# DLRM tower with a three-layer CIN: cur0's sums as six fp32 products and one fp32r product, and the next x transposed at other slots

## Chip, cores and metric

One core of one Trainium2 chip. The metric is the device time of one execution in microseconds (us). Engines: PE (TensorE), DVE (VectorE), ACT (ScalarE), POOL (GpSimd), and SP, which issues DMAs only. The page of the profile and the rows below come from one profiled execution.

## The reference, cut to what matters

```python
# B=1024 rows, 39 fields of D=16; e: (1024, 39, 16), gathered from 39 tables
x0 = e; xk = e; outs = []
for W in (f0, f1, f2):                       # (39*39,128), (128*39,128), (128*39,128)
    z = einsum('bfd,bgd->bfgd', x0, xk).reshape(b, f*g, d)
    cur = einsum('bpd,pm->bmd', z, W)        # cur0, cur1, cur2: (b, 128, 16)
    outs.append(cur); xk = cur
z = sum(concatenate(outs, axis=1), axis=-1)  # (b, 384)
h = concatenate([z, dense_ctx], axis=1)      # (b, 400)
h = relu(h @ W_top1 + b_top1)                # 512
h = relu(h @ W_top2 + b_top2)                # 256
y = h @ W_top3                               # (b, 1)
```

All of it is float32. The change concerns cur0 = the sum over pairs (f, g) of x_f x_g f0[f, g]. As x_f x_g = x_g x_f, the kernel adds f0[f, g] and f0[g, f] once and has 39 x 20 pairs in place of 39 x 39: field f with field f + s (mod 39), for the shifts s = 0 to 19.

## The kernel before, in words

**Tiling.** The 1024 rows are 8 batch tiles (bt) of 128 rows. Each has four groups (q = 0 to 3) of 32 rows, so there are 32 groups g (NG), each with 32 x 16 = 512 columns (row, dimension). A group has four tiles j of 128 columns, and a tile ten chunks c, of four fields each (the tenth has three). TensorE goes through the 40 slots s of a group (s = 10 j + c). In each slot it does one chunk of layer 1: `cur0` of the tile against four fields of f1, 512 columns, as three products of high and low fp32r parts (lines 842 to 844). Six PSUM banks go round: ACT scales the chunks c = 0, 2, 4, 5, 7, 8 by x (line 538), and DVE fuses scaling and sum for c = 1, 3, 6, 9 (lines 681 and 688). DVE adds up the tile (lines 700 and 707) into a ring `cur1` of eight tiles.

**What is laid between the chunks**, at slots written out by hand: the G products of the group before (slot 12, line 799), the seven sums of cur0 for the group after (slots 13, 16, 19, 22, 25, 28, 31, `AT_SUM`, line 770), layer 2 (line 806), the MLP, and in groups with q = 2 the transposes of the next batch tile's x (c = 5 of each tile, so slots 5, 15, 25 and 35, line 744) which ACT reads (line 504). At slot 39 stand the transposes that make x a scale per partition (line 757, ACT line 509).

**cur0.** The partitions hold three blocks of 39 fields (117 rows). Block j of `base` is x moved by -7 j. Copy k (k = 0 to 6) is x moved by k. Their product holds the shifts k, k + 7 and k + 14, so that seven K-tiles cover the 20 shifts (the seventh has two blocks, 78 rows). To make x movable, `x_seq` has 123 rows: the 39 fields three times and six of them once more. SP issues for each group three copies to `base` and six to `shifted` (lines 315 and 324), all from SBUF to SBUF. GpSimd multiplies `shifted` by `base` (line 427) into a ring of three `pairs`, seven times per group, laid between its gathers of the rows of the next batch tile (line 391): three in tile 0, two in tile 1, two in tile 2. TensorE multiplies them by `f0_sum` in fp32 (line 770) into the bank C. In the fourth tile ACT rounds C to the high part of cur0 (line 515), and DVE takes the low part and the sum over the dimension (lines 656 and 658). For group 0 DVE makes the pairs (line 652).

**Queues around it.** GpSimd also copies the gathered rows in field order (line 405), in groups with q = 1: two parts ahead of its pairs in the third tile and two in the fourth. `pair` waits for the sum that frees its place in the ring. SP waits with a copy until the pairs that read the old one are made, and at q = 0 until ACT has read all four transposes of the new x (`x_read`).

## Time and profile before

| | us |
|---|---|
| median of 3 runs | 1350.27 (1345.81 to 1350.93) |
| the profiled execution | 1340.59 |
| its span, first to last instruction | 1338.9 |

| engine | busy us of the span |
|---|---|
| PE | 1274.2 |
| PE weight loads | 979.7 |
| DVE | 1079.9 |
| ACT | 1050.2 |
| POOL | 662.8 |

The granted TensorE clock has a mean of 0.983 of full speed and is below 0.95 only in the first tenth of the span. How to read it: the rows until about 83 us are start (gathers, weights, cur0 of group 0), then come the 32 groups, and the last 20 us are the tail of layer 2 and the MLP. In a timeline, matmuls are pipelined and their ends are modelled, so only the distance from start to start is a price. Idle time of an engine stands in brackets with what ended it.

### The profile page before, as it was taken

To read this page: it belongs to the slowest core of one execution; us is meant where nothing else is said; L and a number is where in the kernel's file an instruction comes from. 1 tells how busy PE (TensorE), PEld (TensorE's weight loads), DVE (VectorE), ACT (ScalarE), POOL (GpSimd) and SP (SyncE) were. 2 spreads that over 40 slices of the span, in tenths; PEclk is the share of its full clock that TensorE was granted. 3 is DMA by queue.
4 is the path that set the end of the run, shared out by engine and by line. 5 is a ranking of instruction groups with operands and counts; after the bars stand their busy time and mean duration, and the time that the engine had idled before them with its cause. 6 is when DMAs were issued, how large, how long until landed. Compare 5 with 4: busy or idle time off the path is not lost. (4 is left out here: it accounts for less than half of the span.)

```text
span 1338.9 us, 21410 instructions
## 1 busy us (share of the span) xinstructions
PE 1274.2 (95%) x6680; PEld 979.7 (73%) x6680; DVE 1079.9 (81%) x2285; ACT 1050.2 (78%) x3363; POOL 662.8 (50%) x634
## 2 busy tenths in 40 slices
PE   1389999999999999999999999999999999999998
PEld 0357777777787777777777777777777777777787
DVE  2059989988889888788878888898887888788884
ACT  2058888888888888788878888888887888788884
POOL 7787556654545557454466545455474532233100
PEclk8689999999999999999999999999999999999999
DMA  5073022100311013110211103111031102110000
GB/s 142 11 196 98 21 58 67 52 28 3 104 33 38 28 29 88 44 32 14 73 51 51 29 3 98 32 44 29 20 90 50 31 13 70 49 49 27 1 1 1
DMA packets 51177, 63.60 MB, mean 48 GB/s; under 512 B 13067, under 2 KB 24344, under 8 KB 51019
## 3 DMA queue, kind: packets, MB, share of 16 engines
q1 hardware_dynamic: 34544, 56.08, 13.7%
q0 software_dynamic: 10128, 2.98, 2.1%
q10 hardware_dynamic: 6392, 3.18, 0.9%
q8 instruction: 53, 0.87, 0.3%
q14 instruction: 60, 0.49, 0.1%
HBM read 11.08 MB, written 1.02 MB: 9 GB/s over the span
## 5 line engine op out<-in xcount | busy, mean ns | idle before, releaser
L538 ACT ACTIVATE scaled_x<-Y,x_col 128x128 f32<-128x128 f32 x3072 | 929.8, 506 | 190.4 <-PE Y L844 178.8
L842 PE MATMUL Y<-f_high,cur_high 128*128 128x512 f32 (+1 forms) x1280 | 603.9, 472 | 3.7 <-DVE sum_b L688 2.0
L844 PE MATMUL Y<-f_high,cur_low 128*128 128x512 f32 (+1 forms) x1280 | 499.1, 390 | 0.0
L843 PE MATMUL Y<-f_low,cur_high 128*128 128x512 f32 (+1 forms) x1280 | 499.0, 390 | 0.0
L427 POOL TENSOR_TENSOR pairs<-shifted,base 117x512 f32<-117x512 f32 x186 | 241.8, 1302 | 435.9 <-PE C L770 434.0
L688 DVE SCALAR_TENSOR_TENSOR sum_a<-Y,x_col,sum_a 128x128 f32<-128x128 f32 x768 | 264.8, 345 | 155.6 <-PE Y L844 153.4
L391 POOL DMA_INDIRECT rows<-in_tbl_dram,ids_sb x312 | 306.6, 983 | 77.5 <-issue 65.9
L842 PEld LDWEIGHTS Y<-f_high,cur_high 128*128 128x128 f32 x1280 | 241.3, 189 | 95.8 <-issue 37.2
L843 PEld LDWEIGHTS Y<-f_low,cur_high 128*128 128x128 f32 x1280 | 242.2, 189 | 86.2 <-issue 52.1
L707 DVE TENSOR_REDUCE cur<-scaled_x 128x128 f32<-128x1920 f32 x128 | 275.6, 2153 | 15.0 <-ACT scaled_x L538 1.6
L844 PEld LDWEIGHTS Y<-f_high,cur_low 128*128 128x128 f32 x1280 | 240.7, 188 | 51.1
L770 PE MATMUL C<-pairs,f_sum 117*128 117x512 f32 (+1 forms) x448 | 236.1, 610 | 5.5 <-DVE pairs L652 5.0
L700 DVE TENSOR_REDUCE scaled_x<-scaled_x 128x128 f32<-128x1536 f32 x128 | 223.4, 1745 | 0.0
L688 DVE SCALAR_TENSOR_TENSOR sum_b<-Y,x_col,sum_b 128x128 f32<-128x128 f32 x640 | 219.2, 342 | 0.0
L770 PEld LDWEIGHTS C<-pairs,f_sum 117*128 117x128 f32 (+1 forms) x448 | 83.0, 193 | 40.6 <-ACT G L521 13.0
L806 PEld LDWEIGHTS C<-G,f_sb 128*128 128x128 f32 x624 | 82.6, 191 | 6.4 <-DVE G L718 0.8
L806 PE MATMUL C<-G,f_sb 128*128 128x128 f32 x624 | 83.3, 275 | 0.7 <-ACT G L521 0.7
L427 POOL TENSOR_TENSOR pairs<-x_seq,base 117x512 f32<-117x512 f32 x31 | 40.0, 1289 | 76.3 <-DMA base<-x_seq 75.2
L688 DVE SCALAR_TENSOR_TENSOR scaled_x<-Y,x_col,sum_b 128x128 f32<-128x128 f32 x128 | 59.8, 467 | 0.0
L688 DVE SCALAR_TENSOR_TENSOR scaled_x<-Y,x_col,sum_a 128x128 f32<-128x128 f32 x128 | 57.7, 451 | 0.0
L681 DVE TENSOR_SCALAR sum_a<-Y,x_col 128x128 f32<-128x128 f32 x128 | 43.9, 343 | 5.7 <-PE Y L844 5.7
L681 DVE TENSOR_SCALAR sum_b<-Y,x_col 128x128 f32<-128x128 f32 x128 | 43.8, 342 | 0.0
(90 smaller groups left out, 730.6 us busy)
## 6 DMA issues: line engine op xcount, KB each, us to landing
shifted<-x_seq SPq DMA_DIRECT2D x157, 234.0 KB
base<-x_seq SPq DMA_DIRECT2D x95, 78.0 KB
rows<-in_tbl_dram,ids_sb POOLq DMA_INDIRECT x312
shifted<-x_seq SPq DMA_DIRECT2D x31, 156.0 KB
G<-in_L_rec_f_dram ACTq DMA_DIRECT2D x3, 832.0 KB, 8.6
w_sb<-in_W_top_dram SPq DMA_DIRECT2D x1, 768.0 KB
f_ext<-in_L_rec_f_dram SPq DMA_DIRECT2D x1, 760.5 KB
w_sb<-in_W_top_dram SPq DMA_DIRECT2D x1, 512.0 KB
```

Source lines behind the costliest of these rows:

```text
L391: pool.indirect_dma_start(out=rows[:, f * D:(f + 1) * D], out_offset=None, in_=tables[f], in_offset=bass.IndirectOffsetOnAxis(ap=ids_sb[:, ...
L427: pool.tensor_tensor(pairs[0:r, z % RING, :], shift, base[0:r, g % 2, :], ALU.mult)\
L538: ins = act.activation(scaled_x[:, :, PLACE[c] + i], where[:, i * M:(i + 1) * M], ACT.Copy, scale=x_col[:, t // JT % QG, t % JT, f:f + 1])
L681: dve.tensor_scalar(acc, src, x, None, ALU.mult).then_inc(acc_steps, 1)
L688: dve.scalar_tensor_tensor(to, src, x, acc, ALU.mult, ALU.add).then_inc(acc_steps, 1)
L700: dve.tensor_reduce(scaled_x[:, :, FIRST_SUM], scaled_x[:, :, 0:HALF], AX.X, ALU.add).then_inc(acc_steps, 1)
L707: dve.tensor_reduce(cur1[:, t % CUR1_RING, :], scaled_x[:, :, FIRST_SUM:PLACES], AX.X, ALU.add).then_inc(acc_steps, 1)
L770: pe.matmul(C[:], f0_sum[0:r, k, :], pairs[0:r, z % RING, :], start=k == 0, stop=k == K0 - 1).then_inc(cur0_summed, 1)
L806: ins = pe.matmul(C[:, 0:P], f2_sb[:, f, :], half[:, f, :], start=f == first, stop=f == end - 1)
L842: pe.matmul(where, ch, wh, start=True, stop=False)
L843: pe.matmul(where, ch, wl, start=False, stop=False)
L844: pe.matmul(where, cl, wh, start=False, stop=True).then_inc(y_filled, 1)
```

## The change

cur0 of group g (from 1 on) is made from six K-tiles and one further product:

- Block j of `base` is now moved by -6 j, and copies k = 0 to 5 give the shifts 0 to 17 with 117 rows. The shifts 18 and 19 are left.
- Rows 117 to 127, 11 rows which were free, hold a part of them: in the copies k = 0 to 3 they carry the pairs of fields 21 to 31 with fields k to k + 10, which are 18 or 19 apart. `x_seq` and `rows_seq` grow to 128 rows, `base` gets a fourth copy (11 rows).
- The last 40 pairs (four runs of ten) are gathered in `base_left` and `left_pairs` by eight copies of ten rows; once these have landed, four copies of 40 rows repeat them twice: 120 rows. GpSimd multiplies them ("left"), ACT rounds them to fp32r (`left_high`, slot 24), GpSimd puts the low part in rows 0 to 39 ("low"). Against them stand f0 as high, high, low. So one fp32r product gives low x high + high x high + high x low. It takes the place of the seventh sum (slot 31).
- GpSimd's order is now three pairs in tile 0, three in tile 1, "left" and "low" in tile 2. The ring of pairs goes on through groups with six uses (`ring_uses`).
- In group 0 the shifts 18 and 19 are a seventh fp32 product with 78 rows, from two copies that GpSimd issues.
- At the start SP loads f0 in 22 DMAs in place of 10, ACT loads 24 pieces for the last product, and DVE makes its high and low parts in four operations.
- The transposes of the next x go from slots 5, 15, 25, 35 to 5, 15, 19, 23 (`AT_X`), and ACT's reads with them.
- For room in SBUF, the ring of `cur1` has 6 tiles and not 8, and DVE waits at each of its tiles for the G product that read the old one; `y`, `z2` and `y_col` lie in `h1`, `h2` and `block`.

```diff
-K0 = -(-SHIFTS // BLK)
+KT = SHIFTS // BLK
+FAR = BLK * KT
+K0 = KT + 1
+EXTRA = P - SEL
+FAR_TILES, FAR_FIELD = 4, NF - FAR
+ROWS = [P - k if k < FAR_TILES else SEL for k in range(KT)]
+FIRST_ROWS = [SEL] * KT + [2 * NF]
+LEFT_FIELD, LEFT_PARTNER, LEFT_RUNS = EXTRA, EXTRA + FAR, 4
+LEFT_N = FAR_FIELD - LEFT_FIELD
...
-AT_X = 5
+AT_MLP2 = 5
+AT_X = (5, 15, 19, 23)
+AT_LEFT_HIGH = 24
-CUR1_RING = 2 * JT
+CUR1_RING = JT + 2
...
                 if g >= 3:
-                    sp.wait_ge(pairs_ready, K0 * (g - 2))
+                    sp.wait_ge(pairs_ready, KT * (g - 2))
...
                 for j in range(BLK):
                     base_copy(sp, g, j)
-                for k in range(1, K0):
+                sp.dma_start(base[SEL:P, g % 2, :], cols[FAR_FIELD:FAR_FIELD + EXTRA, :]).then_inc(based[g % 2], 16)
+                for k in range(1, KT):
                     if g >= 2:
-                        sp.wait_ge(pairs_ready, K0 * (g - 2) + k + 1)
+                        sp.wait_ge(pairs_ready, KT * (g - 2) + k + 1)
                     shift_copy(sp, g, k)
+                if g >= 2:
+                    sp.wait_ge(left_low_ready, g - 1)
+                for r in range(LEFT_RUNS):
+                    rows_r = slice(LEFT_N * r, LEFT_N * (r + 1))
+                    f, v = LEFT_FIELD, LEFT_PARTNER + r
+                    sp.dma_start(base_left[rows_r, :], cols[f:f + LEFT_N, :]).then_inc(left_copied, 16)
+                    sp.dma_start(left_pairs[rows_r, :], cols[v:v + LEFT_N, :]).then_inc(left_copied, 16)
+                sp.wait_ge(left_copied, 16 * (LEFT_COPIES * (g - 1) + 2 * LEFT_RUNS))
+                for j in (1, 2):
+                    rows_j = slice(j * LEFT_PAIRS, (j + 1) * LEFT_PAIRS)
+                    sp.dma_start(base_left[rows_j, :], base_left[0:LEFT_PAIRS, :]).then_inc(left_copied, 16)
+                    sp.dma_start(left_pairs[rows_j, :], left_pairs[0:LEFT_PAIRS, :]).then_inc(left_copied, 16)
...
+            def left_products(g):
+                pool.wait_ge(left_copied, 16 * LEFT_COPIES * g)
+                pool.tensor_tensor(left_pairs[:], left_pairs[:], base_left[:], ALU.mult).then_inc(left_made, 1)
+
+            def left_low(g):
+                n = LEFT_PAIRS
+                pool.wait_ge(left_high_ready, g)
+                pool.tensor_tensor(left_x[0:n, :], left_pairs[0:n, :], left_x[0:n, :].bitcast(F32), ALU.subtract)\
+                    .then_inc(left_low_ready, 1)
...
-                    ks = ((0, 1, 2), (3, 4), (5, 6), ())[j] if g + 1 < NG else ()
+                    ks = ((0, 1, 2), (3, 4, 5), ("left", "low"), ())[j] if g + 1 < NG else ()
...
+            def left_high(g):
+                act.wait_ge(left_made, g)
+                if g >= 2:
+                    act.wait_ge(cur0_summed, K0 * g)
+                act.activation(left_x[:], left_pairs[:], ACT.Copy).then_inc(left_high_ready, 1)
...
-                        if c == AT_X:
-                            if q == 2 and bt + 1 < BT:
-                                read_transposes(bt + 1, j)
-                            if with_mlp:
-                                relu2(mlp, mlp + 1)
+                        if CH * j + c in AT_X and q == 2 and bt + 1 < BT:
+                            read_transposes(bt + 1, AT_X.index(CH * j + c))
+                        if CH * j + c == AT_LEFT_HIGH and g + 1 < NG:
+                            left_high(g + 1)
+                        if c == AT_MLP2 and with_mlp:
+                            relu2(mlp, mlp + 1)
...
-                if j == 0 and g >= 2:
-                    dve.wait_ge(s_filled, S_USE["G", g - 2] + 1)
+                if t >= CUR1_RING:
+                    dve.wait_ge(s_filled, S_USE["G", (t - CUR1_RING) // JT] + 1)
...
+            dve.wait_ge(left_f0_in, 16 * 6 * LEFT_RUNS)
+            dve.tensor_tensor(left_f0[:, 0, :], left_f0[:, 0, :], left_f0[:, 1, :], ALU.add).then_inc(left_f0_ready, 1)
+            dve.wait_ge(left_f0_ready, 1)
+            dve.tensor_copy(f0_left[:], left_f0[:, 0, :]).then_inc(left_f0_ready, 1)
+            dve.wait_ge(left_f0_ready, 2)
+            dve.tensor_tensor(f0_left[64:LEFT, :], left_f0[64:LEFT, 0, :], f0_left[64:LEFT, :].bitcast(F32),
+                              ALU.subtract).then_inc(left_f0_ready, 1)
+            dve.wait_ge(left_f0_ready, 3)
+            dve.tensor_copy(f0_left[64:2 * LEFT_PAIRS, :], left_f0[64:2 * LEFT_PAIRS, 0, :]).then_inc(left_f0_ready, 1)
...
                 if k == 0 and g:
                     pe.wait_ge(c_read, C_USE["sum", g])
-                if g:
-                    pe.wait_ge(pairs_ready, z - K0 + 1)
+                if g and k == KT:
+                    pe.wait_ge(left_low_ready, g)
+                    if g == 1:
+                        pe.wait_ge(left_f0_ready, 4)
+                    w, x = f0_left[:], left_x[:]
                 else:
-                    pe.wait_ge(first_pairs, k + 1)
-                r = K0_ROWS[k]
-                pe.matmul(C[:], f0_sum[0:r, k, :], pairs[0:r, z % RING, :],
-                          start=k == 0, stop=k == K0 - 1).then_inc(cur0_summed, 1)
+                    if g:
+                        pe.wait_ge(pairs_ready, KT * (g - 1) + k + 1)
+                        r = ROWS[k]
+                    else:
+                        pe.wait_ge(first_pairs, k + 1)
+                        r = FIRST_ROWS[k]
+                    w, x = f0_sum[0:r, k, :], pairs[0:r, RING_USE[g, k] % RING, :]
+                pe.matmul(C[:], w, x, start=k == 0, stop=k == K0 - 1).then_inc(cur0_summed, 1)
...
-                    if c == AT_X and q == 2 and bt + 1 < BT:
-                        transposes(bt + 1, j)
+                    if s in AT_X and q == 2 and bt + 1 < BT:
+                        transposes(bt + 1, AT_X.index(s))
```

## Rows read from the trace of the kernel before

**Rows 1.** The page's first part: busy us (share of the span), instructions.
```profile
PE 1274.2 (95%) x6680; PEld 979.7 (73%) x6680; DVE 1079.9 (81%) x2285; ACT 1050.2 (78%) x3363; POOL 662.8 (50%) x634
```
**Rows 2.** Windows: stretch, length, busy of PE, PEld, DVE, ACT, POOL; PEclk, DMA, GB/s.
```profile
680.00:720.00 40.00, 40.00 (x220) 31.27 (x219) 33.07 (x70) 32.84 (x109) 20.66 (x21) 1.00 0.15 41
```
**Rows 3.** Waits, weight loads in 130 to 1285, GpSimd in all: total, times, longest.
```profile
PEld Y L842 <- DVE sum_b L688: 4.1, 11, 1.1
...
POOL pairs L427 <- DMA base<-x_seq: 75.2, 7, 17.0
```
**Rows 4.** Timeline of TensorE, a group with q = 1: start, us, operation.
```profile
603.28 1.02 PE L770 MATMUL C<-pairs,f_sum 117*128 117x512 f32 x2
603.74 0.80 PE L842 MATMUL Y<-f_high,cur_high 128*128 128x512 f32 x1
604.38 0.40 PE L843 MATMUL Y<-f_low,cur_high 128*128 128x512 f32 x1
604.61 0.40 PE L844 MATMUL Y<-f_high,cur_low 128*128 128x512 f32 x1
...
606.06 1.02 PE L770 MATMUL C<-pairs,f_sum 78*128 78x512 f32 x2
606.52 0.79 PE L842 MATMUL Y<-f_high,cur_high 128*128 128x512 f32 x1
607.15 0.40 PE L843 MATMUL Y<-f_low,cur_high 128*128 128x512 f32 x1
```
**Rows 5.** Timeline of GpSimd, the same group.
```profile
592.73 1.30 POOL L427 TENSOR_TENSOR pairs<-shifted,base 117x512 f32<-117x512 f32 x1 [0.53 <-PE C L770]
...
595.46 0.95 POOL L391 DMA_INDIRECT rows<-in_tbl_dram,ids_sb  x1 [0.31 <-issue]
597.73 2.52 POOL L405 COPY rows_seq<-rows 128x624 f32<-128x624 f32 x2 [1.33 <-DMA rows<-in_tbl_dram,ids_sb]
```
**Rows 6.** Timeline of ACT, the same group, tiles 2 and 3.
```profile
599.12 2.71 ACT L538 ACTIVATE scaled_x<-Y,x_col 128x128 f32<-128x128 f32 x8 [0.97 <-PE Y L844]
602.09 2.70 ACT L538 ACTIVATE scaled_x<-Y,x_col 128x128 f32<-128x128 f32 x8 [0.25 <-PE Y L844]
605.04 2.53 ACT L538 ACTIVATE scaled_x<-Y,x_col 128x128 f32<-128x128 f32 x8 [0.26 <-PE Y L844]
607.34 0.67 ACT L515 ACTIVATE cur_high<-C 128x512 fp32r<-128x512 f32 x1
```
**Rows 7.** Timeline of TensorE: sums 1 and 2, and the next group's first product.
```profile
591.63 1.02 PE L770 MATMUL C<-pairs,f_sum 117*128 117x512 f32 x2
...
594.59 1.02 PE L770 MATMUL C<-pairs,f_sum 117*128 117x512 f32 x2
...
613.36 1.05 PE L806 MATMUL C<-G,f_sb 128*128 128x128 f32 x8
```
**Rows 8.** Timeline of DVE: tile 2's sum, and its read of C in tile 3.
```profile
606.68 2.15 DVE L707 TENSOR_REDUCE cur<-scaled_x 128x128 f32<-128x1920 f32 x1
...
611.41 0.69 DVE L658 TENSOR_REDUCE z<-C 128x32 f32<-128x512 f32 x1
```
**Rows 9.** Timeline of TensorE, the group with q = 3: the sum at slot 31.
```profile
683.82 1.02 PE L770 MATMUL C<-pairs,f_sum 78*128 78x512 f32 x2
```
**Rows 10.** Timeline of ACT, the same group: slots 22 and 24.
```profile
676.88 2.71 ACT L538 ACTIVATE scaled_x<-Y,x_col 128x128 f32<-128x128 f32 x8 [0.97 <-PE Y L844]
```
**Rows 11.** Timeline of SP's queue, the copies for the next batch tile's first group.
```profile
652.12 2.35 SPq L315 DMA_DIRECT2D base<-x_seq  x3
```
**Rows 12.** Timeline of GpSimd: the pair that waited for these copies.
```profile
656.23 1.29 POOL L427 TENSOR_TENSOR pairs<-x_seq,base 117x512 f32<-117x512 f32 x1 [9.61 <-DMA base<-x_seq]
```
**Rows 13.** Timeline of DVE at the start.
```profile
60.00 0.72 DVE L631 COPY rows_seq<-rows 128x624 f32<-128x624 f32 x1 [30.88 <-DMA rows<-in_tbl_dram,ids_sb]
...
82.11 0.69 DVE L656 TENSOR_TENSOR cur_low<-C,cur_high 128x512 fp32r<-128x512 f32 x1 [3.66 <-ACT cur_high L515]
```
**Rows 14.** Timeline of ACT at the start.
```profile
60.00 1.31 ACT L487 ACTIVATE rows_seq<-rows 128x624 f32<-128x624 f32 x1 [38.21 <-DMA rows<-in_tbl_dram,ids_sb]
```

More of the change, by code:

```diff
@@ L29, with ring_uses @@
 BLK = P // NF
-K0 = -(-SHIFTS // BLK)
-K0_ROWS = [NF * sum(k + K0 * j < SHIFTS for j in range(BLK)) for k in range(K0)]
+KT = SHIFTS // BLK
+FAR = BLK * KT
+K0 = KT + 1
 SEL = BLK * NF
-SEQ = SEL + K0 - 1
-ROW_PARTS = [(0, NF), (NF, NF), (2 * NF, NF), (SEL, SEQ - SEL)]
+ROW_PARTS = [(0, NF), (NF, NF), (2 * NF, NF), (SEL, P - SEL)]
+EXTRA = P - SEL
[4 more added lines that the diff above has]
+LEFT_N = FAR_FIELD - LEFT_FIELD
+LEFT_PAIRS = LEFT_RUNS * LEFT_N
+LEFT = 3 * LEFT_PAIRS
+LEFT_COPIES = 2 * LEFT_RUNS + 4
 RING = 3
+def ring_uses():
+    uses = [(0, k) for k in range(K0)] + [(g, k) for g in range(1, NG) for k in range(KT)]
+    return {u: n for n, u in enumerate(uses)}, [K0 * g + k for g, k in uses]
 CH = 10
@@ L256, in build @@
         f1_cuts = [13, 26, 39]
-        EXT = NF + K0 - 1
+        EXT = NF + KT - 1
         f0_ext = nc.dram_tensor("f0_ext", (EXT, EXT, M), F32).ap()
-        F0_EXT, F0_LOADS = 3, 2 * (2 * BLK - 1)
+        FAR_RUNS = []
+        for j, (u, v) in enumerate(((0, FAR), (NF - KT, FAR + 1 - KT))):
+            row = 0
+            while row < NF:
+                n = min(NF - row, NF - u, EXT - v)
+                FAR_RUNS.append((NF * j + row, n, u, v))
+                row, u, v = row + n, (u + n) % NF, (v + n) % NF
+        F0_EXT, F0_LOADS = 3, 2 * (2 * BLK - 1) + 2 + 2 * len(FAR_RUNS)
         def extend_f0(eng):
@@ new lines, in load_f0, with load_left_f0 @@
+            for row, n, u, v in FAR_RUNS:
+                eng.dma_start(f0_sum[row:row + n, KT, :], f0_rows(u, v, n)).then_inc(f0_in, 16)
+                eng.dma_start(f0_mirror[row:row + n, KT, :], f0_rows(v, u, n)).then_inc(f0_in, 16)
+        def load_left_f0(eng):
+            for j in range(3):
+                for r in range(LEFT_RUNS):
+                    row = j * LEFT_PAIRS + r * LEFT_N
+                    u, v = LEFT_FIELD, LEFT_PARTNER + r
+                    eng.dma_start(left_f0[row:row + LEFT_N, 0, :], f0_rows(u, v, LEFT_N)).then_inc(left_f0_in, 16)
+                    eng.dma_start(left_f0[row:row + LEFT_N, 1, :], f0_rows(v, u, LEFT_N)).then_inc(left_f0_in, 16)
@@ L455, in _ @@
                             take_rows(bt + 1, part)
[L456 removed]
+                    ks = ((0, 1, 2), (3, 4, 5), ("left", "low"), ())[j] if g + 1 < NG else ()
                     for i in range(max(len(ks), len(fs))):
                         if i < len(ks):
[L459 removed]
+                            if ks[i] == "left":
+                                left_products(g + 1)
+                            elif ks[i] == "low":
+                                left_low(g + 1)
+                            else:
+                                pair(g + 1, ks[i])
                         if i < len(fs):
```

130 lines of the change are left out of this document (74 added, 56 removed).

## The prediction

> **What bounds the kernel now.** First the page's busy shares: TensorE is busy for 1274.2 of 1338.9 us, DVE 1079.9, ACT 1050.2, GpSimd 662.8 [rows 1]. A share is an average, so the second view is a stretch in the middle: from 680 to 720 us TensorE is busy for all 40 us at a granted clock of 1.00, while DVE has 7 us, ACT 7 us and GpSimd 19 us free [rows 2]. Third, the waits: between 130 and 1285 us the weight loads waited for DVE at most 1.1 us in one place and 4.1 us in 11 [rows 3]. So from about 83 us on the row of products on TensorE is the time, and what leaves that row shortens the run as long as the others keep up. They have room on average, but not at every moment, and the change spends that room.
>
> **The product that is replaced.** Starts in TensorE's timeline are pitches. Within a chunk an fp32r product of 512 columns and 128 rows follows the last after 604.61 - 604.38 = 0.23 us. From the start of a cur0 sum (603.28) to the second product of the next chunk (604.38) there are 1.10 us, which hold the fp32 sum and one fp32r product: the sum costs 0.87 us. The seventh sum, with 78 rows, costs 607.15 - 606.06 - 0.23 = 0.86 us: rows don't matter, only columns and type [rows 4]. The durations printed (1.02 for two records) overlap their neighbours and aren't used.
> After the change, groups 1 to 31 have six fp32 sums (128 or 117 rows, same price) and one fp32r product of 120 rows and 512 columns. I price it at 0.23, from its nearest row, the fp32r product of 128x512. Bounds: 0.23 below (it can't stream fewer columns) and 0.86 above (no gain, if the switch of type cost all that was saved). I take the lower end, since chunks follow sums in the same manner already and the switch is inside the 0.86. Saved: 31 x (0.86 - 0.23) = 19.5 us. Group 0 keeps seven fp32 products, the seventh with 78 rows as before: 0.
>
> **The new chain beside it.** The fp32r product needs its pairs as high and low parts: GpSimd multiplies (left), ACT rounds at slot 24, GpSimd subtracts (low), TensorE reads at slot 31. On GpSimd two operations replace one of 1.30 us [rows 5], +1.3 us in a group with 19 us free: nothing. On ACT there is one more pass over 512 columns, about 0.67 us like the split of cur0 at 607.34 [rows 6], in a group with 7 us free. But both are waits in queues. Behind ACT's wait stand the scalings of slots 25, 27 and on, which free TensorE's banks and feed DVE; behind GpSimd's wait for ACT stand gathers, copies of rows and the next group's pairs.
> The tightest place is a group with q=1, where GpSimd copies two parts of the next rows before it comes to left. Before: a pair starts 1.10 us after the sum that frees its place (592.73 [rows 5] against 591.63); sum 2 starts at 594.59 [rows 7]; the last gather is issued at 595.46 and the copies begin at 597.73, when it has landed, 1.3 us after its end [rows 5]. After: pair 5 comes ahead of that gather, 595.7 to 597.0; gather 597.1 to 598.1; landed 599.4; two copies, 602.0; left, 603.25. ACT is done with slot 24 at 599.12 + 2.71 = 601.8 [rows 6], waits 1.5 us and rounds until 603.9; low is ready at 605.2. TensorE asks for it at slot 31, at 606.06 [rows 4]: 0.8 us to spare, no direct wait. Indirectly: ACT's slot 28, which ended at 606.2 (half of the eight from 605.04 [rows 6]), ends at about 607.3, so DVE's sum over the tile starts at 607.4 instead of 606.68, and all behind it moves by 0.7 us. DVE's read of C ends at 612.8 instead of 612.1 [rows 8], while TensorE, 0.63 us sooner, wants to begin the next group at 613.36 - 0.63 = 612.7 [rows 7]: 0.1 us of waiting, bounds 0 and 1.5 (ACT's whole wait passed on). For 8 groups 0.8 us, bounds 0 and 12. Group 1 has one gather more in that tile (1.25 us), which uses up the 0.8: 0.4 us more.
> In the other groups no copy stands there. In the one with q=3, slot 31 is at 683.82 and so sum 2 at 672.35; pair 5 until 674.8, one gather, left 675.9 to 677.2; ACT is done with slot 24 at 679.6 [rows 9, 10] and rounds until 680.3, low 681.6. That is 2.4 us to spare for ACT and 2.2 for TensorE, and ACT's gaps of 0.25 us at slots 25 and 28 take up most of the rounding: 0.
>
> **SP's queue.** Per group it issued 9 copies and will issue 21, at 0.78 us each (2.35 for three [rows 11]). The new 12 come in two steps: 8 small copies (10 rows each), a wait for their landing, 4 of 40 rows. From the issue of a copy to GpSimd's release there are 2.5 us (third base copy at 653.7, GpSimd at 656.23 [rows 12]), so the chain takes 8 x 0.78 + 2.5 + 4 x 0.78 + 2.5 = 14.4 us. It starts when low of the group before is done (605) and is wanted one group later at 637 (675.9 less a pitch of 38.9, half of 683.82 - 606.06): 17 us to spare, 0. Behind it in the queue are the base copies of the group after, wanted later still.
> The Trainium skill (DMA: Bandwidth & Descriptors, the sections Rules for kernel authors and Anatomy of one DMA) speaks against this part: transfers under 64 KB are mostly overhead, with about 2.0 us fixed for each, and should be joined. If the twelve came one after another at that price they would take 24 us, an estimate by that page. The 0.78 us between issues in this trace shows that copies overlap.
> Here the moved transposes matter. Their cost on TensorE is the same wherever they stand. With the fourth at slot 35, SP began the next x's copies at 652.12; slot 23 is 12 chunks (0.70 us), three sums and a transposition sooner, 11.4 us, so 640.7. Nine copies, 7 us, and the small ones, 14.4 us, are done at 662, wanted at 675.9. Unmoved it would be 673.5. So the move gives no time itself, it keeps the chain covered. GpSimd's waits for base copies (75.2 us in 7 places [rows 3]) should go; nobody on the path waited for them. The transposes of slot 19 need ACT's read of those of slot 15: bound one pass, 0.67 us x 7, taken as 0. The shorter ring of cur1 (6) makes DVE wait for the products of group g-1 only at the end of the third tile, some 10 us after they were made: 0.
>
> **Start and end.** SP has 12 more loads of f0 (at 0.78 us 9 us) and ACT 24 small ones (19 us); DVE and ACT sat idle until the rows came at 60.00, for 30.9 and 38.2 us [rows 13, 14]: nothing. DVE makes the high and low weights in four small operations where it sat idle for 3.66 us before its split of cur0 [rows 13]: nothing. GpSimd issues three copies for group 0 instead of two: bounds 0 and 0.78, I take 0.3. For group 1, SP begins after the last pair of group 0, at 78.5, and has the small copies in at 99.9; left comes 7.9 us before slot 31, which is near 109, so at 101: 0, though with little to spare. The tail is the same.
>
> **Sum.** 19.5 - 0.8 - 0.4 - 0.3 = 18.0 us. The profiled execution took 1340.59 us (span 1338.9), so it would take 1322.6. The median of the three runs is 1350.27, 9.7 us above it with the same program, which the trace doesn't explain. I forecast against the median: **1332 us**.
>
> **Rivals.** (1) The hand-over GpSimd, ACT, GpSimd is late in the q=1 groups by 1 to 2 us beyond the margin of 0.8: TensorE stands at slot 31 in 8 groups, 8 to 16 us: 1340 to 1348. For it: the copies of rows stand ahead; against: the pieces are measured. (2) The fp32r product is dearer, in itself or by the switch of type inside one accumulation, which no row shows: halfway, at 0.55 us, 10 us are lost, 1342; at 0.86, 1351. (3) Slower: the hand-over is late in every group. The margin at slot 31 is 2.2 us, and once TensorE waits over 0.63 us in each group the kernel is slower than before, so from 2.9 us late on; at 4 us late 31 x 1.8 - 19.5 = +36 us, 1386. It takes a chain of small copies of 34 us and not 14. Against it: 17 us to spare there and 19 us of GpSimd's time free [rows 2].
>
> **How the numbers follow.** Forecast 0.76 (1321 to 1338: the sum against the profiled execution and against the median, with stalls of 0 to 6 us), rival 1 0.11, rival 2 0.08, rival 3 0.05. The range of 1321 to 1343 takes in half of rivals 1 and 2. A measurement of this kernel tells about 0.5% (6.8 us) from no change: under 1343.5 lie the forecast, over half of 1 and half of 2, 0.87; same 0.08; slower 0.05.
>
> **What would show it.** In the changed profile: starts around the seventh product 0.23 us apart; slot 31 to slot 31 over two groups 76.5 us (77.76 before); no wait of TensorE for GpSimd at slot 31; a wait of ACT of 1 to 2 us before the rounding in q=1 groups alone; none of GpSimd for base copies; chunks starting at 83 us still. Wrong it is if TensorE waits at slot 31, if ACT's wait shows in all groups, or if the seventh product is well over 0.23.

## The result, and the profile after

The changed kernel takes **1360.27 us** (median of 7 runs, 1355.68 to 1364.74); the kernel before, on the same chip, 1346.62 us (7 runs, 1344.99 to 1353.85). The ratio is **1.0092 [1.0071, 1.0113]**: slower, by about 12 to 14 us, where 18 us of gain were forecast. The profiled execution of the changed kernel took 1355.68 us, with a span of 1354.0 us (1340.59 and 1338.9 before).

The page's first part of the changed kernel (busy us, share of the span, instructions), to be read beside [rows 1]:

```profile
PE 1268.2 (94%) x6649; PEld 975.1 (72%) x6649; DVE 1080.0 (80%) x2290; ACT 1053.5 (78%) x3394; POOL 706.4 (52%) x666
```

TensorE has less work and the span is 15.1 us longer, so TensorE must have stood still. Its timeline around slot 31 of a group shows first that the product is not at fault (start, us, operation; starts are pitches):

```profile
663.50 0.39 PE L958 MATMUL Y<-f_high,cur_low 128*128 128x512 f32 x1
663.73 0.40 PE L885 MATMUL C<-left_x,f_left 120*128 120x512 f32 x1
663.97 0.40 PE L956 MATMUL Y<-f_high,cur_high 128*128 128x512 f32 x1
```

The next product starts 663.97 - 663.73 = 0.24 us after it, against 0.86 for the sum it replaces [rows 4]. The waits between 130 and 1285 us (total, times, longest) say where TensorE stands:

```profile
POOL pairs L501 <- DMA shifted<-x_seq: 51.6, 9, 12.2
...
ACT left_x L612 <- POOL left_pairs L506: 25.3, 7, 11.4
...
POOL rows_seq L479 <- DMA rows<-in_tbl_dram,ids_sb: 18.8, 7, 5.1
...
PE C L885 <- POOL left_x L511: 9.0, 1, 9.0
```

One stop of 9.0 us at slot 31, ACT late seven times, and a line that the forecast had not thought of: GpSimd waits 51.6 us in nine places for a copy to `shifted`. (The waits of its pairs for copies to `base` [rows 3] are gone but for one of 1.7 us, as forecast.) To place the loss I took the starts of the transposes of slot 39 (the chunks' groups end there) in both timelines and subtracted the distances:

| stretch, after minus before, us | profiled run | same kernel, later set |
|---|---|---|
| up to the first chunks (81 us) | +2.2 | -1.0 |
| group 0 | +3.0 | +3.7 |
| group 1 | +13.4 | +13.1 |
| the seven later groups with q = 1 | +2.0 | +2.2 |
| the other 21 groups from group 2 to 29 | -6.6 | -9.5 |

So the change works in most groups (about 0.5 to 0.6 us each), loses in the groups with q = 1, and loses most in two groups at the start. (Of the seven later groups with q = 1 six lose 0.4 to 0.5 us each; the seventh belongs to the last batch tile, has no next rows to copy, and gains 0.55.) The stretch before the chunks differs by some us between executions of kernels with the same code in it (-3.2 to +5.5 in the runs below), and I explain nothing by it.

**Group 1.** SP's queue in the changed kernel, the copies for group 1's pairs (start, us in the queue):

```profile
82.61 0.74 SPq L414 DMA_DIRECT2D base<-x_seq  x1
83.39 8.80 SPq L379 DMA_DIRECT2D shifted<-x_seq  x5
92.23 0.73 SPq L424 DMA_DIRECT2D base_left<-x_seq  x1
```

Five copies take 8.80 us to issue. Half of that is the second one, of 126 rows, which stands behind the one of 127 rows:

```profile
84.09 4.27 SPq L379 DMA_DIRECT2D shifted<-x_seq  x1
```

In the kernel before six of them at the same place take 4.79, that is 0.80 each:

```profile
80.93 4.79 SPq L324 DMA_DIRECT2D shifted<-x_seq  x6
```

What moved in the meantime stands in the DMA view, in 40 equal parts of the stretch 84 to 90 us (digits: busy tenths of the 16 DMA engines), first the changed kernel, then the kernel before in 84 to 97 us:

```profile
DMA  3120100001000200001013313010000005686885
GB/s 68 41 24 4 41 14 14 14 27 14 0 0 27 27 0 0 0 27 27 0 27 44 41 31 34 27 34 27 27 27 27 27 14 164 191 246 218 287 273 123
```
```profile
DMA  4587787788979837999999999999999999999999
GB/s 140 126 251 252 246 284 284 233 265 277 265 240 103 76 107 230 290 323 347 334 290 302 296 284 302 284 309 290 290 290 301 295 254 284 291 296 290 265 287 259
```

After the first slice, for almost 5 us, the 16 engines move 0 to 44 GB/s between them, though a copy of 254 KB is under way and four more wait to be issued; before, 230 to 347 GB/s are usual (weights among them). In the stretch 84.7 to 89.0 us the same view gives for SP's queue (packets, MB, share of the 16 engines):

```profile
q1 hardware_dynamic: 36, 0.07, 6.4%
```

6.4% of 16 engines is one engine. The copy of 127 rows was issued at 83.39, and GpSimd, which waits for nothing else, can use it 14 us later (timeline of GpSimd, groups 0 and 1; in brackets the idle time and what ended it):

```profile
97.38 1.29 POOL L501 TENSOR_TENSOR pairs<-shifted,base 127x512 f32<-127x512 f32 x1 [7.39 <-DMA shifted<-x_seq]
...
136.92 1.30 POOL L501 TENSOR_TENSOR pairs<-shifted,base 127x512 f32<-127x512 f32 x1 [8.04 <-DMA shifted<-x_seq]
...
156.80 2.40 POOL L479 COPY rows_seq<-rows 128x624 f32<-128x624 f32 x2 [5.08 <-DMA rows<-in_tbl_dram,ids_sb]
159.17 1.25 POOL L506 TENSOR_TENSOR left_pairs<-left_pairs,base_left 120x512 f32<-120x512 f32 x1
161.16 1.26 POOL L511 TENSOR_TENSOR left_x<-left_pairs,left_x 40x512 fp32r<-40x512 f32 x1 [0.74 <-ACT left_x L612]
```

254 KB in 14 us are 19 GB/s. The pairs that GpSimd makes in group 1 come late too. Its copies for them stand in SP's queue behind the loads of the weights of layer 2 and the MLP; they go out at 119.53 us, and in a kernel that loads these weights two groups later (weights_later, below) at 102.59:

```profile
119.53 2.47 SPq L370 DMA_DIRECT2D base<-x_seq  x3
```
```profile
102.59 2.35 SPq L370 DMA_DIRECT2D base<-x_seq  x3
```

Then the copy of 127 rows takes its 14 us again, and GpSimd idles 8.04 us for it. So the last gather is issued late and lands late, and behind it stand the two copied parts of the next rows, then left, ACT's rounding and low. ACT waits 11.4 us with the banks of Y full, and TensorE stands:

```profile
160.45 0.63 ACT L612 ACTIVATE left_x<-left_pairs 120x512 fp32r<-120x512 f32 x1 [11.39 <-POOL left_pairs L506]
```
```profile
162.48 0.80 PE L885 MATMUL C<-left_x,f_left 120*128 120x512 f32 x1 [9.04 <-POOL left_x L511]
163.07 0.63 PE L956 MATMUL Y<-f_high,cur_high 128*128 128x512 f32 x1
163.50 0.63 PE L957 MATMUL Y<-f_low,cur_high 128*128 128x512 f32 x1
```

The stop has a second price. After it products follow each other by 163.50 - 163.07 = 0.43 us instead of 0.23: TensorE's clock had fallen to its lower level (1.2 GHz) while it stood; from 163 to 167 us the granted clock is 0.50. The windows (stretch; length, busy of PE, PEld, DVE, ACT, POOL; granted clock, DMA share, GB/s) show that, and the weights of layer 2 and the MLP in the first line:

```profile
110.00:120.00 10.00, 8.73 (x36) 6.21 (x35) 7.60 (x16) 7.74 (x28) 8.42 (x9) 1.00 1.06 304
...
150.00:160.00 10.00, 3.44 (x14) 2.22 (x12) 3.77 (x8) 0.00 (x0) 4.62 (x5) 0.84 0.36 106
160.00:170.00 10.00, 7.52 (x23) 5.97 (x24) 5.64 (x13) 8.79 (x31) 8.92 (x10) 0.65 0.14 39
```

**The groups with q = 1.** GpSimd, ACT, and TensorE at the start of the next group, in the group that answers to [rows 5 to 7]:

```profile
614.66 0.98 POOL L465 DMA_INDIRECT rows<-in_tbl_dram,ids_sb  x1
617.93 2.48 POOL L479 COPY rows_seq<-rows 128x624 f32<-128x624 f32 x2 [2.29 <-DMA rows<-in_tbl_dram,ids_sb]
620.37 1.28 POOL L506 TENSOR_TENSOR left_pairs<-left_pairs,base_left 120x512 f32<-120x512 f32 x1
622.40 1.30 POOL L511 TENSOR_TENSOR left_x<-left_pairs,left_x 40x512 fp32r<-40x512 f32 x1 [0.74 <-ACT left_x L612]
```
```profile
621.69 0.63 ACT L612 ACTIVATE left_x<-left_pairs 120x512 fp32r<-120x512 f32 x1 [2.32 <-POOL left_pairs L506]
```
```profile
625.65 2.15 DVE L804 TENSOR_REDUCE cur<-scaled_x 128x128 f32<-128x1920 f32 x1 [1.55 <-ACT scaled_x L635]
```
```profile
628.89 0.50 PE L956 MATMUL Y<-f_high,cur_high 128*128 128x512 f32 x1 [0.42 <-DVE sum_a L785]
```

This is the forecast chain, link by link: copies of rows, left, ACT's wait, DVE's late sum over the tile, TensorE at the group's end.

### The profile page after: what moved, and what is told of

Read it like the earlier page. It is cut to its first block and busy times, and to the rows that moved or that the text cites. A ratio compares the mean times of both kernels' runs of the same rounds, so it can differ in the third digit from the quotient of the medians.

```text
span 1354.0 us, 21824 instructions
## 1 busy us (share of the span) xinstructions
PE 1268.2 (94%) x6649; PEld 975.1 (72%) x6649; DVE 1080.0 (80%) x2290; ACT 1053.5 (78%) x3394; POOL 706.4 (52%) x666
## 3 DMA queue, kind: packets, MB, share of 16 engines
q1 hardware_dynamic: 44009, 68.76, 17.2%
## 5 line engine op out<-in xcount | busy, mean ns | idle before, releaser
L956 PE MATMUL Y<-f_high,cur_high 128*128 128x512 f32 (+1 forms) x1280 | 593.9, 464 | 10.4 <-DVE sum_b L785 5.9
L501 POOL TENSOR_TENSOR pairs<-shifted,base 117x512 f32<-117x512 f32 (+3 forms) x155 | 201.6, 1302 | 411.8 <-PE C L885 349.8
L465 POOL DMA_INDIRECT rows<-in_tbl_dram,ids_sb x312 | 309.7, 993 | 73.4 <-issue 56.9
L885 PE MATMUL C<-pairs,f_sum 117*128 117x512 f32 (+4 forms) x386 | 204.7, 614 | 6.3 <-DVE pairs L749 5.6
L885 PEld LDWEIGHTS C<-pairs,f_sum 117*128 117x128 f32 (+4 forms) x386 | 71.2, 193 | 39.4 <-ACT G L618 13.1
L511 POOL TENSOR_TENSOR left_x<-left_pairs,left_x 40x512 fp32r<-40x512 f32 x31 | 39.9, 1288 | 68.1 <-ACT left_x L612 68.1
L487 POOL TENSOR_SCALAR x_block<-x_col,half_block 128x160 f32<-128x160 f32 x64 | 43.5, 693 | 0.7
```

The lines of the kernel that those rows point to most:

```text
L465: pool.indirect_dma_start(out=rows[:, f * D:(f + 1) * D], out_offset=None, in_=tables[f], in_offset=bass.IndirectOffsetOnAxis(ap=ids_sb[:, ...
L501: pool.tensor_tensor(pairs[0:r, z % RING, :], shift, base[0:r, g % 2, :], ALU.mult)\
L885: pe.matmul(C[:], w, x, start=k == 0, stop=k == K0 - 1).then_inc(cur0_summed, 1)
L956: pe.matmul(where, ch, wh, start=True, stop=False)
```

## The experiments

**Theory A**: the copy k = 1 to `shifted`, 127 rows, is carried by very few DMA engines, and what stands behind it is late. It came from the DMA view above and from a rule I had not weighed. The Trainium skill (DMA: Bandwidth & Descriptors, section "Why a DMA increments its semaphore by 16 and not by 1") says that a copy uses the largest number of engines up to 16 that divides the sizes of its slowest dimensions, 127 partitions being one of its examples for a single engine. By that rule 126 rows get 14, 125 rows 5, 117 rows 13, and 113, a prime, one. Rivals: the weights loaded in group 1 (B), the copied rows ahead of left in q = 1 (C), a cost of the change that has nothing to do with copies (D).

Ratios are against the kernel before on the same chip. The kernels came in four sets, each on a chip of its own.

### Set 1: one part at a time, and all

```diff
 # split_copies
-eng.dma_start(shifted[0:r, k - 1, :], cols[k:k + r, :]).then_inc(done, 16)
+eng.dma_start(shifted[0:min(r, SEL), k - 1, :], cols[k:k + min(r, SEL), :]).then_inc(done, 16)
+if r > SEL:
+    eng.dma_start(shifted[SEL:r, k - 1, :], cols[k + SEL:k + r, :]).then_inc(done, 16)
...
 # weights_later: layer 2's and the MLP's weights
-                if g == 1:
+                if g == 3:
...
```

`SEL` is 117. GpSimd waits for both parts of a split copy; that line is left out here and below.

> The changed kernel, with the copies k = 1, 2, 3 of groups 1 on issued as two DMAs each: 117 rows, and the other 10, 9 or 8 rows. Same bytes, three DMAs more per group. Theory A (a copy of 127 rows goes over one DMA engine, one of 125 over five, one of 117 over thirteen): the second copy is issued in under 1 us instead of 4.7; in group 0 GpSimd no longer waits 7.4 us for a shifted copy; group 0 costs 35 us instead of 38, and group 1 loses 6 to 9 of its 13.4 us. Time 1350 us (10 us less than the changed kernel). Rival B (the weights of f2 and the MLP, issued 20 us later than before, are what holds up group 2's copies): group 0 may gain, group 1 keeps its 13 us; time 1357. Rival C (only the place of the gathers and row copies ahead of left): no change beyond 1 us.

Measured: 1335.5 us (1332.78 to 1340.11), **0.9933 [0.991, 0.9956]**. Three more DMAs in each group turn the slower kernel into a faster one.

> The changed kernel, with the loads of f2 and of the MLP weights issued in SP's pass for group 3 instead of group 1. Theory B (their backlog holds up group 2's copies): GpSimd's wait of 8.0 us for a shifted copy in group 1 goes, pairs 1 to 5 come 8 to 10 us sooner and group 1's 13.4 us shrink to 2 or less; time 1347. Theory A (the 127-row copy on one DMA engine is slow by itself): a wait of 3 to 5 us for it stays in group 1 and 7 us in group 0, group 1 still loses 4 to 6 us; time 1351.

Measured: 1344.35 us, 1.0012 [1.0, 1.0024]. GpSimd still waits for the long copy (42.5 us in eight places from 130 us on), but group 1 costs +6.4 instead of +12.8 to +13.4. The weights take part in the loss.

```diff
 # left_first: q = 1, GpSimd's order in tiles 2 and 3
-                    if q == 1 and j >= 2 and bt + 1 < BT:
-                        for part in ((0, 1), (2, 3))[j - 2]:
+                    if q == 1 and j == 3 and bt + 1 < BT:
+                        for part in (2, 3):
                             take_rows(bt + 1, part)
...
                                 left_products(g + 1)
+                                if q == 1 and bt + 1 < BT:
+                                    take_rows(bt + 1, 0)
                             elif ks[i] == "low":
                                 left_low(g + 1)
+                                if q == 1 and bt + 1 < BT:
+                                    take_rows(bt + 1, 1)
```

> The changed kernel, with GpSimd's work in the third tile of q = 1 groups in the order left, first row copy, low, second row copy (instead of both row copies ahead of left). Theory C (the hand-over in q = 1 groups is late because left stands behind the landing of the gathers): ACT's waits of 2.3 us for left go, each q = 1 group costs 0.6 us less than before the change instead of 0.4 more, 7 us over seven groups; and group 1, where left waited for the gathers until 156.8, gains 5 to 8 us more. Time 1347. If the q = 1 cost has another reason (DVE's order, the row copies in tile 3), the groups stay at +0.4 and the time at 1358 or more.

Measured: 1339.88 us, 0.9974 [0.9963, 0.9985]. The seven later q = 1 groups go from +2.0 to -3.9 in sum, 1.0 us in each of the six that copy rows; group 1 still costs +10.3.

> The three edits together: split copies, weights in SP's pass for group 3, left ahead of the row copies. If these three causes are all, every group from 1 on costs 0.6 us less than before the change, group 0 about 0.5 more than before or the same, and the kernel takes 1331 us, 1.1 to 1.4 per cent less than the kernel before. If something else takes time (the start 2 us later, the tail, the longer SP queue), it stays at 1337 or above.

Measured: 1327.45 us (1325.53 to 1328.45), **0.9882 [0.9861, 0.9904]**. It beats both kernels.

### Set 2: repeats and isolations on another chip

> The changed kernel unaltered, on the chip of the next three, to compare them with. Expected 0.9 per cent slower than the kernel before, as in the first comparison: 3 us in group 0, 13 us in group 1. The first rows of the page so far also differed in where the chunks start (78 to 83 us in kernels whose start is the same code), so I expect to see 2 to 5 us of that here.

Measured: 1355.93 us, 1.0065 [1.004, 1.009]. Groups 0 and 1 cost +4.6 and +12.8, as before.

> The changed kernel with only the copy k = 1 (127 rows) as two DMAs of 117 and 10 rows; the copies of 126 and 125 rows stay whole. Theory A1 (it is the one DMA engine under 127 rows; 126 rows go over fourteen and 125 over five): nearly all of the gain of the three splits, time within 3 us of that kernel (0.994 of before), and SP's second copy issued in under 1 us. Rival A2 (any copy over 117 rows is slow, or the 125 rows over five engines count as much): half of the gain or less, 1.000 to 1.005 of before.

Only the copy with k = 1 is split (`if g and k == 1:`, 117 and 10 rows). Measured: 1354.99 us (1345.57 to 1360.93), 1.005 [1.0024, 1.0076]: the wait of GpSimd's pairs for these copies went from 51.6 us to 0.9, and the time hardly moved. Some of its groups with q = 3 cost +1.1 to +1.2. This spoke against A, and the isolations that follow came out 1.0059 as well, so I suspected the chip as much as the theory.

In the kernel before, the copy k = 1 to `shifted` (117 rows) is sent as 113 and 4 rows:

```diff
-            eng.dma_start(shifted[0:r, k - 1, :], cols[k:k + r, :]).then_inc(done, 16)
+            if k == 1 and g:
+                eng.dma_start(shifted[0:113, 0, :], cols[1:114, :]).then_inc(done, 16)
+                eng.dma_start(shifted[113:r, 0, :], cols[114:1 + r, :]).then_inc(done, 16)
+            else: ...
```

> The kernel before, with its copy k = 1 (117 rows) of groups 1 on issued as two DMAs of 113 and 4 rows: same bytes, one DMA more, 113 being a prime. Theory A (how the number of rows divides sets the engines that a copy uses): the copy behind it is issued in 4 to 5 us instead of 0.76, GpSimd waits 6 to 8 us for a shifted copy in group 0 and again in group 1, where the weights' loads are in the way; 2 to 6 us slower than before, since pairs come late but the ring gives some slack. Rival (not the row count but the 128-row bounds or the new 12 copies make it slow): issue stays at 0.76 us each and the time within 1 us of before.

Measured: 1354.25 us, 1.0059 [1.0037, 1.008].

All three amendments, with the seventh product in fp32 (only its precision changes):

```diff
-                    w, x = f0_left[:], left_x[:]
+                    w, x = f0_left[:].bitcast(F32), left_x[:].bitcast(F32)
```

> The kernel with the three edits, with its seventh product read as fp32 in place of fp32r: the same 120 rows and 512 columns, the same chain on SP, GpSimd and ACT. It measures what the cheaper product is worth once the stalls are gone. Theory: 0.63 us per group, 31 groups, 19.5 us more than with fp32r, so 1.002 to 1.005 of before. If DVE or ACT has become the limit of the groups, less: 5 to 10 us.

Measured: 1355.67 us, 1.0059 [1.0039, 1.008]: 0.0177 above all_three of set 1, and the product's own price would be 0.0145 (19.5 us).

### Set 3: the copies again, the amendments in pairs, the transposes

> The three long copies of the pairs (127, 126, 125 rows) each go as 117 and 10, 9 or 8 rows; nothing else differs from the changed kernel. Run again so that it shares a chip with the next one. Against the kernel before it was 0.9933 [0.991, 0.9956]. Theory A (the copy of 127 rows goes through one DMA engine and everything behind it is late): again 0.991 to 0.996, with no wait of GpSimd for a copy of more than 0.7 us. If the first gain was chance of the chip (rival): 0.999 or more.

Measured: 1334.62 us, 0.9941 [0.9922, 0.996].

> Only the copy of 127 rows is split; those of 126 and 125 rows stay whole. Run before it was 1.005 [1.0024, 1.0076] on another chip, though GpSimd's wait for the copies was gone. Theory A1 (the copy of 127 rows alone does the harm): the same as the kernel with three copies split, within 0.002. Theory A2 (copies of 125 rows, that is 5 engines, and of 126 rows, 14 engines, do harm of their own, through other transfers behind them): dearer by 0.004 or more than the kernel with three copies split, on the same chip.

Measured: 1338.09 us (1333.6 to 1339.77), **0.9956 [0.9942, 0.9971]**. A1 holds here: the 127 rows do nearly all the harm. The 3.5 us between this and the kernel above (intervals overlap) may be the 125 and 126 rows' share; in the profiles groups 0 and 1 differ by 1.5 and 2.7 us. The trace of this run holds when each copy had landed: that of 125 rows 4.8 to 6.8 us after its issue, that of 126 rows 3.0 to 3.8, that of 117 rows mostly 3.1 to 3.4. The same program was 1.005 in set 2, 0.9% higher.

> Three copies split, and in the q=1 groups the rows 0 to 9 of the next tile are copied after left and low; the weights of f2 and the MLP are loaded in group 1 as in the changed kernel. The kernel with the weights moved to group 3 as well gave 0.9882 [0.9861, 0.9904], that with the copies split alone 0.9933. If the q=1 hand-over costs 1.0 us in each of its seven later groups (0.4 - -0.56), this is 7 us under the split one: 0.988. If the weights loaded in group 1 still matter once the copies are short, it stays at 0.990 or above; if not, it equals 0.988.

Measured: 1326.2 us, 0.9881 [0.9861, 0.9902], the same as with the weights moved too (0.9882 and 0.9874, on other chips). In the profiles of both kernels group 1 costs 0.0: with the copies short, the weights in group 1 cost nothing that shows.

```diff
 # old_transposes: all three amendments, and
-AT_X = (5, 15, 19, 23)
+AT_X = (5, 15, 25, 35)
```

> The kernel with all three amendments, but the four transposes of the next x back at slots 5, 15, 25 and 35 instead of 5, 15, 19 and 23. The prediction had the chain of small copies done at 673.5 and wanted at 675.9, so 2.4 us to spare and no cost: 0.988, as with the transposes moved. Rival (the chain is longer than reckoned, and the base copies need the time too): GpSimd waits for the copies in every fourth group, 1 to 5 us of waiting in 7 groups, 0.99 to 1.01.

Measured: 1326.03 us, 0.9879 [0.9859, 0.9899]. GpSimd waits for the copies to `base` again (49.6 us in 7 places), and once the groups run nobody waits for GpSimd. Its timeline for one of them, and the left product of the same group, before which it isn't idle, and then SP's queue with the last of the small copies that it needs:

```profile
648.10 1.29 POOL L504 TENSOR_TENSOR pairs<-x_seq,base 128x512 f32<-128x512 f32 x1 [6.06 <-DMA base<-x_seq]
...
666.35 0.98 POOL L467 DMA_INDIRECT rows<-in_tbl_dram,ids_sb  x1 [0.15 <-issue]
667.36 1.32 POOL L509 TENSOR_TENSOR left_pairs<-left_pairs,base_left 120x512 f32<-120x512 f32 x1
```
```profile
662.84 0.72 SPq L432 DMA_DIRECT2D left_pairs<-left_pairs  x1
```

The last copy is out at 663.56 and left begins at 667.36. With the 2.5 us from the issue of a copy to GpSimd's release by [rows 12] that is 1.3 us to spare.

### Set 4: what the product and the copy are worth, on one chip

> The changed kernel again, as the anchor of this set. It was 1.0092 [1.0071, 1.0113] and 1.0065 [1.004, 1.009] on two chips: 1.004 to 1.011 here.

Measured: 1350.4 us, **1.0056 [1.0038, 1.0074]**.

> The kernel with the copies split, the left products before the copied rows and the weights in group 3, again: 0.9882 [0.9861, 0.9904] before. If the gain is the kernel's and not one chip's, 0.986 to 0.991 here too.

Measured: 1325.67 us (1323.46 to 1328.41), **0.9874 [0.9853, 0.9895]**.

> The kernel with all three amendments, with the seventh product as fp32 instead of fp32r (same tiles, same 120 rows; that product alone is in another precision). Measured once on another chip: 1.0059 [1.0039, 1.008], where a kernel repeated elsewhere had come out 0.009 higher. If the product is worth its own 19.5 us and nothing else: 0.988 + 0.0145 = 1.003. If TensorE's slower row also ran into waits on DVE and ACT, as the first measurement has it: 1.005 or more. If the first was the chip's doing and the product is worth less than its price: 1.000 or below.

Measured: 1343.75 us (1339.97 to 1344.99), **1.0004 [0.9993, 1.0016]**. Against all_three_b on the same chip the fp32r product is worth 1343.75 - 1325.67 = 18.1 us. The rest of the change, with the amendments, costs nothing that can be told: 1.0004. The 1.0059 of set 2 was not the kernel's alone.

> The kernel before with one base copy of 117 rows sent as 113 and 4 rows (113 is prime, so one DMA engine carries it, if the rule of the divisor holds); nothing else of the change. Measured once: 1.0059 [1.0037, 1.008]. Theory A (a one-engine copy ahead of the gathers and of the other copies costs by itself): again 1.003 to 1.009. If that chip was the cause: within 0.002 of 1.

Measured: 1352.03 us (1346.08 to 1353.73), **1.0058 [1.0037, 1.0079]**, as in set 2. So one copy with a prime number of rows costs a tuned kernel 8 to 10 us, with nothing else of the change in it. Its queue and its GpSimd show the same signature, though this copy is 8 KB shorter than the one it replaces:

```profile
81.68 0.65 SPq L325 DMA_DIRECT2D shifted<-x_seq  x1
82.37 2.65 SPq L326 DMA_DIRECT2D shifted<-x_seq  x1
```
```profile
95.65 1.28 POOL L431 TENSOR_TENSOR pairs<-shifted,base 117x512 f32<-117x512 f32 x1 [8.03 <-DMA shifted<-x_seq]
```
```profile
POOL pairs L431 <- DMA shifted<-x_seq: 69.3, 7, 10.8
...
PEld C L774 <- POOL pairs L431: 7.6, 7, 2.7
```

The copy of 4 rows issued behind it takes 2.65 us to get out, where 0.8 is usual, and the pair comes 14.0 us after the issue at 81.68. In 83.0 to 85.5 us SP's queue has 6.2% of the 16 engines' time, again one engine. TensorE waits for pairs in seven places; the groups with q = 3 cost +0.4 to +2.5.

The distances between the group ends, as in the first table, for the kernels that carry the argument (us, minus the kernel before):

| | to the chunks | group 0 | group 1 | 7 x q = 1 | other 21 | at the last |
|---|---|---|---|---|---|---|
| changed (after_third) | -1.0 | +3.7 | +13.1 | +2.2 | -9.5 | +8.6 |
| weights_later | -2.8 | +4.4 | +6.4 | +2.0 | -9.7 | +0.3 |
| left_first | -2.2 | +4.7 | +10.3 | -3.9 | -10.8 | -2.0 |
| split_k1_b | -2.3 | +1.0 | +4.0 | +2.1 | -8.9 | -4.1 |
| split_copies_b | -1.7 | -0.5 | +1.3 | +2.1 | -8.9 | -7.7 |
| split_and_left | -2.2 | -0.5 | 0.0 | -3.9 | -9.8 | -16.5 |
| all_three_b | -3.0 | -0.5 | 0.0 | -3.9 | -9.7 | -17.2 |
| left_fp32_b | -1.9 | +1.6 | 0.0 | +0.4 | +1.3 | +1.4 |
| before_prime_b | +2.3 | +1.5 | 0.0 | +0.1 | +6.2 | +10.1 |

From after_third to all_three_b there are 25.8 us: 17.3 in groups 0 and 1, 6.1 in q = 1, 2.0 before the chunks and 0.2 in the rest (25.6; the tenths are rounded). The medians are 24.7 us apart.

## Why the prediction was wrong, point by point

**The product: right.** 0.24 us measured for 0.23, and 18.1 us between the medians for 19.5. In all_three_b 25 of the 28 groups from 2 to 29 gain about 0.6 us each. Groups 2 and 4 gain nothing (0.0) and group 3 comes out 0.4 us longer; there TensorE waits for DVE where it did not before. The waits from 149 to 223 us, all_three_b and then the kernel before:

```profile
PE Y L963 <- DVE sum_b L792: 1.9, 2, 1.2
```
```profile
PE Y L842 <- DVE sum_b L688: 0.4, 2, 0.2
```

**SP's queue: this step failed.** The forecast priced the nine copies to `base` and `shifted` at 0.78 us each, by three copies to `base` with 39 rows each [rows 11]; the kernel before has none but 39, 78 and 117 rows. Three of them now have 127, 126 and 125 rows, and these numbers stand in the diff (`ROWS`). I looked at the count of the copies and at their bytes, not at the number of rows. In the changed kernel the five copies to `shifted` took 8.80 us to issue in place of 3.9, and the first one landed 14 us after its issue, not 2.5. That the cause is the copy and not its neighbourhood is shown by split_k1_b (0.9956 where the changed kernel has 1.0056 to 1.0092) and by before_prime_b (1.0058 with a copy of 113 rows). That it is the number of engines is the skill's rule, and the traces agree. They hold every increment of a copy's semaphore. Each copy brings one early, at its issue, and the others as its parts land: 13 for 117 rows (kernel before), 14 for 126, 5 for 125, one for 127 (after_third), and 5 for the copies of 113 and 4 rows together (before_prime_b). These are the engines that the rule gives. The copy of 127 rows has landed 13.6 to 15.3 us after its issue in every group where the trace has its increment, and the copy of 126 rows behind it, on 14 engines, not before 13.6 us either; with the 127 rows split it lands after 3.0 to 3.8 (split_k1_b). Length alone can't explain that: 113 rows, fewer than before, behave as 127 do, and 117 with 10 do not. On the small copies: the 2.0 us that I took from the skill stand there, in the section that I named, for DMAs that GpSimd issues, and these twelve are issued by SP; the sum did not use them.

**The start: this is where the failure was paid.** I had "the small copies in at 99.9, wanted at 101" for group 1. The pairs of group 1 began 7.4 us late at 97.38, the small copies were issued until 106.1 and left came at 110.9 (then without a wait for them); in split_copies_b SP ended them at 97.9. And the weights of layer 2 and the MLP, to whose move I gave no price, went out at 107.5 instead of 87.2 in the kernel before, with 304 GB/s in 110 to 121 us, and held the queue until 119.4, where the copies for group 2's pairs stood behind them. GpSimd then waited 8.04 us once more, and TensorE stood for 9 us and came back at the lower clock: +13 us in one group. The weights alone are not the cause (with short copies, moving them gains nothing: 0.9881 and 0.9882), and without them the long copy still costs 6.4 us in that group.

**The hand-over in q = 1: mechanism right, size too small.** Forecast: ACT waits 1.5 us, DVE's sum over the tile 0.7 us late, 0.1 us per group, bounds 0 and 1.5. Measured: ACT waits 2.3 us, DVE's sum 1.5 us late (625.65, less the 17.49 us by which this group lies later by GpSimd's fourth pair, 607.27 against 589.78; so 608.16 against 606.68 [rows 8]), and the group loses 1.0 us, 6.1 us in the six groups that copy rows (+2.2 against -3.9; the seventh, in the last batch tile, copies none). The term that was mis-sized is the landing of the last gather: 1.3 us of idleness by [rows 5] were carried over, 2.3 were found in each of the six. The likely reason is that pair 5 now comes before that gather, so that the gather and SP's 234 KB copy, which waits for that pair, are in flight together; the traces show the two together, but no run tested it. The 0.8 us of margin went into that. left_first takes it all back.

**The transposes, the small copies, the ring of cur1, ACT's and DVE's extra work: right, at 0.** Moving the transposes back changes nothing (0.9879, against 0.9882 and 0.9874 for the same kernel with them moved, on other chips). The forecast gave 2.4 us to spare without the move; 1.3 are found.

**The sum.** 18.0 us were forecast. The kernel with the amendments, in which the queue and the hand-over cost what the forecast gave them, is 15.1 us (set 1), 16.5 and 16.7 (set 3) and 16.7 (set 4) faster than before. The changed kernel itself lacks 24.7 us of that in set 4.

**The rivals.** Rival 1 (q = 1) happened, but smaller than its range: 6.1 us for 8 to 16, at the group's end rather than at slot 31. Rival 2 did not happen. Rival 3 had the right sign and the wrong place: it asked for a hand-over that is late in every group by a long chain of small copies. What happened is one long copy that is late, deadly in the one group where GpSimd has no lead, and in the steady groups hidden by the lead of a whole group. My chance of 0.05 for slower came from having asked only how many copies there are. No row showed a copy of 125 to 127 rows, so its price should have been bounded from both sides; with the upper end open, this edit could not have been put down at 0.

**What stays open.** Set 2's chip gave split_k1_only and left_fp32 ratios of 1.005 and 1.0059, sets 3 and 4 gave the same programs 0.9956 and 1.0004, while the changed kernel and before_prime came out alike on both. In split_k1_only's profile four of the groups with q = 3 are 1.1 to 1.2 us longer than in the kernel before, where split_k1_b's are 0.6 shorter, and the chunks start 5.5 us later. What the traces of set 2 do show is that ACT and DVE stand where they don't on the other chips. In left_fp32 five groups with q = 2 are 0.7 to 0.8 us longer than in the kernel before, and in each ACT idles 3.0 to 3.2 us before a scaling in the last tile; DVE idles 2.00 us beside it, though TensorE's products start at their usual distance. The first line is left_fp32, the second the same place in left_fp32_b:

```profile
976.01 1.30 ACT L642 ACTIVATE scaled_x<-Y,x_col 128x128 f32<-128x128 f32 x4 [3.01 <-PE Y L965]
```
```profile
962.55 0.79 ACT L642 ACTIVATE scaled_x<-Y,x_col 128x128 f32<-128x128 f32 x2 [0.52 <-PE Y L965]
```

In split_k1_only ACT has such a stop, of 1.7 to 1.9 us, just ahead of TensorE's stall in each of the four long groups. What holds the two engines up there is not shown, and so set 2's ratios for these two kernels remain unexplained.

Group 0 costs +3.0 to +4.7 in the changed kernel and -0.5 to +1.0 when all three long copies are split. In the profiled run two things make it up: left is late there too, ACT waits 3.19 us for it and TensorE 1.27 us at slot 31, and the first products follow each other by 0.43 us for some 3 us, about 1.6 us lost to the lower clock. In weights_later TensorE waits 2.8 us for a pair at 95.13 instead. So the late pairs reach TensorE in different places from run to run.

```profile
114.73 0.51 PE L885 MATMUL C<-left_x,f_left 120*128 120x512 f32 x1 [1.27 <-POOL left_x L511]
```

## What to carry to other kernels

Look at the number of partitions of every SBUF-to-SBUF copy, not only at its bytes: a number with a large divisor up to 16 (117, 78, 39, 10) was issued here in 0.7 to 0.8 us, and 117 rows had landed after some 3.1 to 3.4; 125 rows took 4.8 to 6.8 to land; a prime number (127, 113) held the queue for up to 5 us longer and landed after 12 to 15. Two copies, of 117 and 10 rows, were cheaper than one of 127. Then ask where a late transfer meets the least lead: it is the first groups, where loads are still running and the engine that makes the inputs is not yet a group ahead. A stop of TensorE of some us there (9.0 us here, 4.0 in weights_later) was paid twice, since it came back at the lower clock.

## What the runs showed of the hardware that I had not expected

- A copy of 254 KB with 127 rows moved at 19 GB/s (14 us from issue to use), with the 16 engines together at 0 to 44 GB/s over almost 5 us, and the issue of the copy behind it took 4.27 us meanwhile. 226 KB with 113 rows: 14.0 us.
- A copy's semaphore increments, less the early one, count the engines that the rule gives: 13 for 117 rows, 14 for 126, 5 for 125, one for 127. A copy on 14 engines landed no sooner than the one on a single engine ahead of it (13.6 us and more, 3.0 to 3.8 without it).
- TensorE's granted clock was 0.84 in the 10 us in which it stood (150 to 160 us) and 0.65 in the next 10; in 163 to 167 us it was 0.50, and 512-column products came 0.43 us apart for 0.23.
- The wait for a gather's landing was 2.3 us where one copy of 234 KB was in flight beside it, and 1.3 before.
- The time from the start to the first chunks varied by 8.7 us (-3.2 to +5.5) between profiled executions of kernels with the same code there, and one chip gave two of the four kernels repeated elsewhere ratios 0.6 to 0.9% higher.
